# Vision tower, expert stage: score halves in groups of 16 experts, spreads of three blocks together, gathers of five blocks in one piece

## The reference

```python
logits = jnp.einsum('bsd,ed->bse', x, gate_w)
top_logits, indices = jax.lax.top_k(logits, TOP_K)          # 6 of 64
scores = jax.nn.softmax(top_logits, axis=-1)
lattice_out = sum over the six of  scores * (x @ lattice_weights[expert])
h = x + lattice_out @ out_w.T + out_b
out = (h - mean) * rsqrt(var + eps) * ln_g + ln_b
```

## Time and profile before

| | us |
|---|---|
| median of 3 runs | 1736.97 |
| lowest, highest run | 1724.95, 1737.28 |
| the profiled execution, whole time | 1721.6 |
| its span | 1719.6 |
| the expert stage in it, from the first spread | 209.7 |

### The profile page before, as it was taken

One profiled execution on the slowest core, in us unless ns is written; L12 is line 12 of the kernel. 1 busy time (PEld: TensorE's weight loads), 2 busy tenths in 40 slices (PEclk: granted clock), 3 DMA queues, 4 the chain that ended last, 5 costly groups with the idle time before them and its releaser, 6 DMA issues. The chain is left out here.

```text
span 1719.6 us, 47103 instructions
## 1 busy us (share of the span) xinstructions
PE 1587.7 (92%) x21500; PEld 900.3 (52%) x21500; DVE 1201.3 (70%) x1409; ACT 585.9 (34%) x788; POOL 140.4 (8%) x64
## 2 busy tenths in 40 slices
PE   8799999997999999889999997999988889989996
PEld 3455555555555555555555555777731118833332
DVE  3498989876989898688989886555500008946777
ACT  2432222223222222233222222444478885500000
POOL 1000000000000000000000000000000000067764
PEclk9999999999999999999999999999999999999998
DMA  5133232243665656455555551899986642085551
GB/s 200 66 124 130 118 136 111 118 185 107 246 233 210 239 206 244 148 188 214 228 221 222 225 227 67 297 355 359 362 324 234 228 141 90 16 192 148 141 141 37
DMA packets 64980, 321.48 MB, mean 187 GB/s; under 512 B 18896, under 2 KB 20880, under 8 KB 30992
## 3 DMA queue, kind: packets, MB, share of 16 engines
q1 hardware_dynamic: 39984, 182.97, 31.9%
q10 hardware_dynamic: 24800, 135.51, 19.4%
HBM read 181.08 MB, written 137.36 MB: 185 GB/s over the span
## 5 line engine op out<-in xcount | busy, mean ns | idle before, releaser
L820 ACT ACTIVATE act_c<-slots,conv_b 128x512 f32<-128x512 f32 x512 | 352.3, 688 | 735.4 <-PE slots L540 735.4
L540 PEld LDWEIGHTS slots<-inv_w,inv_out 128*128 128x128 f32 x4096 | 499.4, 196 | 188.2 <-issue 179.0
L540 PE MATMUL slots<-inv_w,inv_out 128*128 128x128 f32 x4096 | 541.7, 287 | 3.2 <-DVE inv_out L715 3.2
L715 DVE STREAM_TRANSPOSE inv_out<-slots 128x1024 f32<-128x1024 f32 x256 | 304.5, 1228 | 99.1 <-PE slots L505 99.1
L691 DVE STREAM_TRANSPOSE turned_h<-slots 128x1024 f32<-128x1024 f32 x200 | 237.9, 1228 | 31.3 <-PE slots L439 30.9
L680 DVE STREAM_TRANSPOSE turned_w<-act_c 128x1024 f32<-128x1024 f32 x192 | 225.3, 1216 | 1.1 <-ACT act_c L820 1.1
L439 PE MATMUL slots<-turned_w,fwd_w 32*64 32x512 f32 x3200 | 198.7, 603 | 3.8 <-DMA turned_w<-in_x_turned_dram 2.6
L1644 POOL TENSOR_TENSOR modes<-at_turned,modes 128x1024 f32<-128x1024 f32 x14 | 34.9, 2498 | 1524.5 <-DMA at_turned<-level_scratch 1509.4
L831 ACT ACTIVATE inv_out<-slots,b 128x1024 f32<-128x1024 f32 x128 | 135.7, 1111 | 21.2 <-PE slots L638 21.2
L451 PE MATMUL slots<-turned_h,fwd_h 64*64 64x320 f32 x1600 | 137.2, 454 | 1.3 <-DVE turned_h L691 1.3
L697 DVE STREAM_TRANSPOSE modes<-slots 128x640 f32<-128x640 f32 x96 | 80.9, 845 | 79.9 <-PE slots L451 79.9
(11 more groups left out here) (151 smaller groups left out, 1021.5 us busy)
## 6 DMA issues: line engine op xcount, KB each, us to landing
act_scratch<-act_c ACTq DMA_DIRECT2D x128, 1024.0 KB, 5.1
act_c<-act_scratch SPq DMA_DIRECT2D x128, 1024.0 KB, 5.2
at_turned<-level_scratch SPq DMA_DIRECT2D x36, 256.0 KB, 4.1
at_ret_t<-level_scratch SPq DMA_DIRECT2D x34, 256.0 KB, 4.0
mode_w<-in_sw_dram SPq DMA_DIRECT2D x20, 320.0 KB, 3.3
xin<-in_x_dram SPq DMA_DIRECT2D x4, 1024.0 KB, 8.4
at_straight<-level_scratch SPq DMA_DIRECT2D x16, 256.0 KB, 4.1
at_crossed<-level_scratch SPq DMA_DIRECT2D x16, 256.0 KB, 4.0
```

Source lines behind the costliest of these rows:

```text
L540: mm = nc.tensor.matmul(banks[:, p, at:at + 128], inv_out[:, t % 2, i, p, :, :, r].rearrange("p b o -> p (b o)"), inv_w[:, i, :], start=Fa ...
L715: nc.vector.transpose(dst, src).then_inc(inv_turned, 1)
L820: nc.scalar.activation(act_c[:, t % RING, :, p, :], banks[:, p, :].rearrange("p (i m) -> p i m", i=2), ACT.Gelu, bias=conv_b[:, l:l + 1]). ...
```

## The change

- The scores' halves are laid out in four groups of 16 experts. A group's 32 rows (16 high, 16 low) are one quarter of the partitions of `halves_t`. A spread's matmul now has 32 rows instead of 128, at partitions 32r to 32r+31, and `select` is 32x128 for each of 8 pairs, repeated in the four quarters: one load and one rounding copy.
- `PAIR_OF` gives each block its pair of experts, so that consecutive VectorE blocks have their rows in different quarters.
- Blocks go in groups of five (three VectorE, two GpSimd). TensorE's loop spreads the next group, first half of its three blocks and then the second halves, and then gathers the five blocks of this group without a spread between them. `spread` is a semaphore for each half.
- WB is 12: four new buffers and the two of `halves`, which are free when the front is over.
- The projection comes after the gather with N % 32 == 5.

```diff
-WB = 6
+WB = 12
-    select = np.zeros((2, EXPERTS, EXPERTS // 2, 2, D), f)
-    for e in range(EXPERTS):
-        select[:, e, e // 2, e % 2, :] = 1.0
+    select = np.zeros((4, 2, EXPERTS // 4, EB // 4, 2, D), f)
+    for e in range(EXPERTS // 4):
+        select[:, :, e, e // 2, e % 2, :] = 1.0
...
+GROUP_OF = 5
...
+def expert_pairs():
+
+    pair_of = {}
+    for g in range(CHUNKS):
+        pairs = iter([EB // 4 * r + n for n in range(EB // 4) for r in range(4)])
+        for pool in (False, True):
+            for N in range(g * EB, (g + 1) * EB):
+                if on_pool(N) == pool:
+                    pair_of[N] = next(pairs)
+    return pair_of
...
-        halves = sb("ex_halves", [128, 2, CT, 2, EXPERTS])
+        halves = sb("ex_halves", [128, 2, CT, 4, 2, EXPERTS // 4])
+        more = sb("ex_weighted", [128, 4, SLOT])
+        weighted += [more[:, b, :] for b in range(4)]
+        weighted += [flat(halves[:, b]) for b in range(2)]
...
-            for c in range(2):
-                load_select(c)
+            sp.dma_start(select_raw[:], k_select).then_inc(select_in, 16)
...
-            for c in range(2, CHUNKS):
-                load_select(c)
...
-            def spread_block(N):
-
-                i, g, n = DVE_BLOCKS.index(N), N // EB, N % EB
-                for half in range(2):
-                    if i >= PB:
-
-                        pe.wait_ge(weigh, 2 * (i - PB) + half + 1)
-                    at = g * SLOT + half * 512
-                    nc.tensor.matmul(slots[:, i % PB, half * 512:(half + 1) * 512],
-                                     select[:, n * 128:(n + 1) * 128], halves_t[:, at:at + 512],
-                                     start=True, stop=True).then_inc(spread, 1)
+            def spread_half(N, half):
+
+                i, g = DVE_BLOCKS.index(N), N // EB
+                if i >= PB:
+
+                    pe.wait_ge(weigh, 2 * (i - PB) + half + 1)
+                at, r = g * SLOT + half * 512, PAIR_OF[N] // (EB // 4)
+                rows = slice(r * 32, (r + 1) * 32)
+                nc.tensor.matmul(slots[:, i % PB, half * 512:(half + 1) * 512],
+                                 select[rows, PAIR_OF[N] % (EB // 4), :], halves_t[rows, at:at + 512],
+                                 start=True, stop=True).then_inc(spread[half], 1)
...
-            for N in DVE_BLOCKS[0:2]:
-                spread_block(N)
+            def spread_group(q):
+
+                for half in range(2):
+                    for N in range(q * GROUP_OF, min((q + 1) * GROUP_OF, BLOCKS)):
+                        if not on_pool(N):
+                            spread_half(N, half)
+
+            spread_group(0)
             for N in range(BLOCKS):
-                if not on_pool(N) and DVE_BLOCKS.index(N) + 2 < len(DVE_BLOCKS):
-                    spread_block(DVE_BLOCKS[DVE_BLOCKS.index(N) + 2])
+                if N % GROUP_OF == 0:
+                    spread_group(N // GROUP_OF + 1)
                 gather(N)
-                if N % EB == 3 and N > EB:
+                if N % EB == 5 and N > EB:
                     project(N // EB - 1)
             project(CHUNKS - 1)
...
-                hi, lo = halves[:, c % 2, :, 0, :], halves[:, c % 2, :, 1, :]
-                link(nc.vector.tensor_copy(hi.bitcast(F32R), level[:, c % 2]))
-                nc.vector.tensor_tensor(lo, level[:, c % 2], hi, ALU.subtract).then_inc(halves_set, 1)
+                hi, lo = halves[:, c % 2, :, :, 0, :], halves[:, c % 2, :, :, 1, :]
+                whole = level[:, c % 2].rearrange("p t (r e) -> p t r e", r=4)
+                link(nc.vector.tensor_copy(hi.bitcast(F32R), whole))
+                nc.vector.tensor_tensor(lo, whole, hi, ALU.subtract).then_inc(halves_set, 1)
...
-                    e, n = FRONT.moved_of("scores", CHUNKS - 1)
+                    e, n = FRONT.moved_of("scores" if N < 6 else "s_turn", CHUNKS - 1)
```

More of the change, by code:

```diff
@@ L903 @@
 ROWS_RING = 6
+GROUP_OF = 5
 def on_pool(N):
-    return N % 5 in (1, 3)
+    return N % GROUP_OF in (1, 3)
 POOL_BLOCKS = [N for N in range(BLOCKS) if on_pool(N)]
 DVE_BLOCKS = [N for N in range(BLOCKS) if not on_pool(N)]
+def expert_pairs():
[7 more added lines that the diff above has]
+    return pair_of
+PAIR_OF = expert_pairs()
 def transformer(nc, slots, ident, front, h_dram, level_dram, gate_t, lattice, out_wt, out_b, ln_g, ln_b, k_select, out):
@@ L953, in transformer @@
         sums = sb("ex_sums", [128, 2, CT])
-        halves = sb("ex_halves", [128, 2, CT, 2, EXPERTS])
+        halves = sb("ex_halves", [128, 2, CT, 4, 2, EXPERTS // 4])
+        more = sb("ex_weighted", [128, 4, SLOT])
+        weighted += [more[:, b, :] for b in range(4)]
+        weighted += [flat(halves[:, b]) for b in range(2)]
         halves_t = sb("ex_halves_t", [128, TOKENS], F32R)
-        select = sb("ex_select", [128, EB * 128], F32R)
-        select_raw = sb("ex_select_raw", [128, 2, SLOT])
+        select = sb("ex_select", [128, EB // 4, 128], F32R)
+        select_raw = sb("ex_select_raw", [128, SLOT])
         mixed = flat(qkv[:])[:, 0:CHUNKS * 512].rearrange("p (g n) -> p g n", n=512)
@@ L966, in transformer @@
         zeroed = sem("ex_zeroed")
-        select_in = [sem(f"ex_select_in{b}") for b in range(2)]
+        select_in = sem("ex_select_in")
         select_set = sem("ex_select_set")
@@ L982, in transformer @@
         moved = {"dve": sem("at_moved_dve"), "act": sem("at_moved_act")}
-        spread = sem("ex_spread")
+        spread = [sem(f"ex_spread{half}") for half in range(2)]
         weigh = sem("ex_weigh")
@@ L1046, in _ @@
             for i, N in enumerate(POOL_BLOCKS):
-                g, n = N // EB, N % EB
+                g = N // EB
                 if i >= ROWS_RING:
@@ L1054, in _ @@
                 for e in range(2):
+                    n = 2 * PAIR_OF[N] + e
                     sp.dma_start(rows_of[i % ROWS_RING][e * D:(e + 1) * D, :],
-                                 level_dram[2 * n + e:2 * n + e + 1, g * SLOT:(g + 1) * SLOT].broadcast_to(
+                                 level_dram[n:n + 1, g * SLOT:(g + 1) * SLOT].broadcast_to(
                                      [D, SLOT])).then_inc(rows_in[i % ROWS_RING], 16)
@@ L1146, in s_turn @@
                 pe.wait_ge(halves_set, c + 1)
-                turn(s, 128, lambda j: flat(halves[:, c % 2, j, :, :]))
+                turn(s, 128, lambda j: flat(halves[:, c % 2, j]))
             def level_turn(c):
@@ L1179, in gather @@
                     mm = nc.tensor.matmul(slots[j * D:(j + 1) * D, SLOTS - 1, g % 2 * 512:g % 2 * 512 + 512],
-                                          lattice_w[:, n, :], weighted[N % WB][:, j * 512:(j + 1) * 512],
+                                          lattice_w[:, PAIR_OF[N], :], weighted[N % WB][:, j * 512:(j + 1) * 512],
                                           start=(n == 0), stop=(n == EB - 1))
@@ L1374, in softmax @@
                     dve.wait_ge(filled, FRONT.filled_at("s_turn", c - 2))
-                hi, lo = halves[:, c % 2, :, 0, :], halves[:, c % 2, :, 1, :]
-                link(nc.vector.tensor_copy(hi.bitcast(F32R), level[:, c % 2]))
-                nc.vector.tensor_tensor(lo, level[:, c % 2], hi, ALU.subtract).then_inc(halves_set, 1)
+                hi, lo = halves[:, c % 2, :, :, 0, :], halves[:, c % 2, :, :, 1, :]
+                whole = level[:, c % 2].rearrange("p t (r e) -> p t r e", r=4)
+                link(nc.vector.tensor_copy(hi.bitcast(F32R), whole))
+                nc.vector.tensor_tensor(lo, whole, hi, ALU.subtract).then_inc(halves_set, 1)
             def weigh_half(N, half):
                 i, g = DVE_BLOCKS.index(N), N // EB
-                dve.wait_ge(spread, 2 * i + half + 1)
+                dve.wait_ge(spread[half], i + 1)
                 if half == 0 and N >= WB:
@@ L1544, in move_level, with round_select @@
                 move("level_turn", c, 0, level_t[:, c % 2, :], rows=D)
-            def round_select(c):
-                act.wait_ge(select_in[c % 2], 16 * (c // 2 + 1))
-                nc.scalar.copy(select[:, c * SLOT:(c + 1) * SLOT], select_raw[:, c % 2, :]).then_inc(select_set, 1)
+            def round_select():
+                act.wait_ge(select_in, 16)
+                nc.scalar.copy(flat(select[:]), select_raw[:]).then_inc(select_set, 1)
             root_x(0)
@@ L1563, in _ @@
             move_qk(0, 1)
-            round_select(0)
+            round_select()
             move_qk(1, 0)
@@ L1567, in _ @@
             root_x(3)
-            round_select(1)
             move_qkv(2, 0)
@@ L1580, in _ @@
             move_qk(2, 1)
-            round_select(2)
             exponent(0)
@@ L1584, in _ @@
             move_qk(3, 1)
-            round_select(3)
             move_s(0)
```

7 lines of the change are left out of this document (1 added, 6 removed).

## The result

| | before | after |
|---|---|---|
| median, us | 1732.62 | 1722.76 |
| lowest, highest run | 1722.82, 1740.09 | 1719.01, 1733.33 |
| runs | 20 | 20 |
| span of the profiled execution | 1719.6 | 1720.0 |
| in it, first spread to the end of the span | 209.7 | 199.2 |

The changed kernel is 9.9 us faster; the ratio is 0.9952, 95% interval 0.9936 to 0.9969.

The account below looks back on a forecast made before the run. TensorE was taken to bound chunk 0, with VectorE close behind in chunks 1 and 2. Terms -11.9 - 2.6 + 4.5 = -10.0 us took 1736.97 to 1727.0 us; own range -18 to -3, overall range 1709 to 1742 (0.8).

Parts of the forecast that it names:

- A group of five blocks at 5.15 us: TensorE, expert stage: three blocks' spreads plus five gathers at 0.86 us take 5.15 us instead of 6.7.
- The spreads of three blocks side by side, taken at 0.85: TensorE: quarters of the array overlap, so three blocks' spreads cost 0.85 us; bounds 0.81 and 1.73.
- Chunk 0, -11.9 us to VectorE's step 0: Chunk 0: VectorE's first finish step starts at 1561.9 instead of 1573.8 us, with GpSimd just keeping up.
- the walk: Chunks 1 to 3: TensorE and VectorE followed in order, group by group; together -2.6 us.
- the clock term: Chunks 1 to 3: TensorE's 1.2 GHz stretch after each chunk's last wait costs 1.5 x 3 = 4.5 us; bounds 0 and 9.
- The coupling by groups: Chunks 1 to 3: TensorE waits for VectorE group by group, some 4 us at a time, about 10 us a chunk.
- the 0.97 us for each lengthened place: VectorE's finish: eight SBUF-only places each wait 0.97 us on average while GpSimd weighs, 7.7 us a chunk.
- WB = 12 doesn't help: Chunks 1 to 3: the three PSUM slots, not the ring, tie VectorE to TensorE; no size given.
- the third rival: Chunks 1 to 3: VectorE never idles, chunks 1 and 2 take its 38 us each; 1705 us; chance 0.15.
- The first, no overlap: TensorE's spreads: the quarters don't overlap, a group's spreads cost 1.73 us; 1738 us; chance 0.15.
- The fourth, GpSimd too slow in chunk 0: Chunk 0: GpSimd or its rows pace it at 2.9 us a weigh, no gain there; 1735 us; chance 0.08.
- The second, GpSimd shutting VectorE out: VectorE's finish: GpSimd's lock lengthens each place, 1741 us at 1.57 us, +22.6 at a whole weigh, 2.33; chance 0.12.

Follow-up runs that it names:

- e1: Changed kernel with TensorE's order of the kernel before (spread by block, two VectorE blocks ahead); ratio to the kernel before 1.0004, stage 208.1 us.
- e2: Changed kernel with pairs reassigned so that consecutive VectorE blocks have their rows in the same quarter of the array; ratio to the kernel before 0.9995, stage 204.8 us.
- e5: Changed kernel with WB = 6 instead of 12, nothing else; ratio to the kernel before 0.9981, stage 207.8 us.
- e4: Changed kernel with VectorE's finish steps after blocks n = 12, 14, ... 28 instead of 8, 10, ... 24; ratio to the kernel before 0.9921, stage 191.5 us.
- e9: Changed kernel where GpSimd, before weighing block N, also waits for VectorE's weigh of block N - 1; ratio to the kernel before 0.9919, stage 193.8 us.
- e6: Changed kernel with finish steps spread evenly, after n = 12, 14, 17, 19, 22, 24, 27, 29, 31; ratio to the kernel before 0.9899, stage 191.1 us.
- e8: Changed kernel with finish steps after n = 12, 14, ... 28 and spreads before a group's fourth gather; ratio to the kernel before 0.9916, stage 192.6 us.

## Why the prediction was right, and where it was not

The forecast of -10.0 us met -9.9, by sum and by direction. (It named 1727.0, from a median of three runs; from the median of 20, 1732.62, the same sum gives 1722.6, against 1722.76.) The mechanism was right in chunk 0. In chunks 1 to 3 errors of about 3 us each cancelled, so that the closeness of the sum is luck.

- **A group of five blocks at 5.15 us:** 5.11. The spreads of three blocks side by side, taken at 0.85, cost 0.67. Right, and for the stated reason (e1, e2).
- **Chunk 0, -11.9 us to VectorE's step 0:** from the first spread to step 0 it was 1573.82 - 1509.92 = 63.9 us before and 1572.25 - 1520.80 = 51.45 after, so -12.5. From gather 1, where the working starts, it was 42.9 us, as forecast; the other 0.5 is that gather 1 came earlier after the first spread. GpSimd kept up: TensorE waited for it only there.

```profile
1529.36 5.39 PE L1191 MATMUL slots<-modes,ex_lattice_w 128*64 128x512 f32 x12 [1.53 <-POOL modes L1660]
```

- **Chunks 1 to 3, -2.6 by the walk, +4.5 for the clock.** From step 0 to step 0 the walk gave 45.5 and 46.8, and 37.3 to the last copy, without the clock term. Measured: 51.6, 46.4 and 36.1 (1572.25, 1623.80, 1670.24, 1706.29). The sum, 134.0, is what walk and clock term gave together, 134.1, but not by these shares: chunks 2 and 3 came out a little below the walk without any clock term, and chunk 1 six above it. The coupling by groups, the least supported step, held. Two terms in it were mis-sized, in opposite directions.
- **The first mis-sized term is the 0.97 us for each lengthened place,** 7.7 us a chunk. I took it as even over the chunks and bounded it by one GpSimd weigh, 2.33. Measured, the finish's operations were lengthened by 9.5, 3.2 and 4.0 us. In chunk 1 one place alone waited 5.5 us; in chunk 2 the two that were lengthened by more than 0.1 waited 3.1 us together (L853 1.13 and L855 2.33, of which 0.17 each is their own). So the walk was too long for chunks 2 and 3 and too short for chunk 1.
- **The second is the clock, taken at 4.5 us.** The windows from step 0 to step 8 of chunks 1, 2 and 3, in the columns of the earlier trace rows, show it far more at its lower level than before:

```profile
1572.25:1601.61 29.36, 19.01 (x70) 6.04 (x72) 26.99 (x33) 0.21 (x1) 17.97 (x9) 0.74 0.57 153
1623.80:1646.98 23.18, 18.82 (x68) 6.06 (x70) 20.70 (x33) 0.21 (x1) 11.72 (x5) 0.73 0.48 136
1670.24:1693.67 23.43, 19.22 (x74) 6.13 (x76) 22.67 (x35) 0.21 (x1) 14.79 (x6) 0.83 0.14 33
```

Its cost shows behind each chunk's last wait for VectorE, where no later wait hides it. These windows run from the end of that wait to the next group's spreads:

```profile
1598.54:1606.17 7.63, 7.63 (x24) 2.38 (x25) 5.52 (x9) 0.00 (x0) 2.41 (x1) 0.66 0.37 103
1641.99:1650.08 8.09, 8.09 (x25) 2.48 (x26) 6.21 (x10) 0.00 (x0) 2.35 (x1) 0.63 0.42 98
1691.34:1698.49 7.15, 7.05 (x24) 2.11 (x24) 4.82 (x8) 0.00 (x0) 1.43 (x1) 0.76 0.16 37
```

At a granted 1.00 a whole group took 5.11 us in chunk 0, so these took 2.5, 3.0 and 2.0 more. An estimate from these rows is some 7 us in all, since VectorE's own weighs might have held one or two of them back by up to 1 us. Without it the three chunks come to about 127 us and the walk said 129.6: the walk was nearly 3 too long and the clock term nearly 3 too short. No run took the clock apart from the waits.

- **"WB = 12 doesn't help":** false. With the new order the ring of 6 loses 8.6 us of stage (e5). My argument looked at VectorE's tie to TensorE through PSUM and left out that, with five gathers in a piece, buffers come free in pieces too.
- **Two slips in the working.** In chunk 3 it names two groups' spreads behind the last wait; its 37.3 counts one, and the kernel has one there. In the third rival "about -32" should be about -35 by its own terms (-10.0 - 16.3 - 4 - 4.5). Neither moves the forecast. And it took 1% as what a measurement can tell; 20 executions of each kernel gave an interval of 0.17% to either side.
- **The rivals.** The first, no overlap, would have shown 1.7 us between runs of gathers and not 0.67. The fourth, GpSimd too slow in chunk 0, would have shown TensorE waiting for it there; it did so once, for 1.5 us. The second, GpSimd shutting VectorE out, was real in chunk 1: one place waited 5.5 us, over its stated bound of 2.33, and the eight places 1.2 on average. It didn't come in 2 and 3 (0.4 and 0.5 on average), where a full ring stopped GpSimd (idle 4.54 and 6.20 us at a time in chunk 2, 6.49 in chunk 3). The third, VectorE never idle, didn't happen: it waited 3.9, 4.4 and 5.7 us for the projection, which e4 then showed to be worth having.

## What to carry to other kernels

Here TensorE's work on a quarter of its rows gained nothing by being smaller (e1), but by standing together, with fewer changes to other work, and next to work in other quarters (e2); group it so, and expect the gain only where TensorE sets the pace. Where another engine is close behind, price its whole chunk first: here VectorE's 37 to 38 us a chunk, a fifth of it waiting for GpSimd, left 0.6 us of gain after chunk 0. And a larger ring also loosens an engine that blocks another one: tie the blocker to the progress of the blocked (e9, one wait), and then move the blocked engine's work to where it has slack.

## What the hardware did that I had not expected

A VectorE operation on SBUF alone can be shut out not for one GpSimd instruction but for a run of them: 5.70 us through three weighs, 9.15 through four, in each of five cases until GpSimd paused. The Trainium skill (SBUF — State Buffer, on who interferes with whom) has the one that issues first hold the shared ports for its whole instruction while the other waits; it doesn't say that the waiting one may be passed over again and again. The measurement decides. It isn't always so: in the kernel before, L1404 took 2.83 us at most, with weighs following each other (it began at 1578.88, the weighs at 1578.81 and 1581.13). All five cases over 5 us are the same one-input TENSOR_SCALAR on 8 elements a partition (L1421, in e6 L1422), in step 1 in chunk 1, while GpSimd had several weighs it could run in a row; no TENSOR_TENSOR of the finish was over 2.9 us in any run. But it isn't the kind of operation alone, nor GpSimd's running on alone. In e5 a TENSOR_SCALAR of the same size ended with the first weigh, though the next followed at once, and in e8's chunk 2 so did L1421 itself (VectorE's line first, then GpSimd's):

```profile
1588.19 2.37 DVE L855 TENSOR_SCALAR ex_stats_o<-ex_stats_o 128x8 f32<-128x8 f32 x1
1588.17 2.37 POOL L1660 TENSOR_TENSOR modes<-at_ret_t,modes 128x1024 f32<-128x1024 f32 x1 [2.93 <-PE slots L1191]
1590.49 2.36 POOL L1660 TENSOR_TENSOR at_centred_y<-at_ret_t,modes 128x1024 f32<-128x1024 f32 x1
...
1632.30 0.64 DVE L1421 TENSOR_SCALAR ex_stats_o<-ex_stats_o 128x8 f32<-128x8 f32 x1
1630.51 2.40 POOL L1660 TENSOR_TENSOR modes<-at_straight,modes 128x1024 f32<-128x1024 f32 x1 [0.76 <-PE slots L1191]
1632.84 2.39 POOL L1660 TENSOR_TENSOR at_qkv<-at_crossed,modes 128x1024 f32<-128x1024 f32 x1
```

What decides whether the operation gets in stays open. e9 shows only that stopping GpSimd there removes the long wait. In e2, with the same ring, L1421 in chunk 1 took 1.60 us; there GpSimd had only that one weigh left before it waited for a gather.
